# The expert stage of an AdaLN block: output groups, selection steps and the last unit's rows are placed elsewhere

## The chip, the cores and the metric

One core of a Trainium2 chip runs the whole program. The metric is the device time of one execution in microseconds. The kernel before has a median of 1168.9 us in three runs (1168.67 to 1169.73).

## The reference

The input is x of shape (4, 2048, 256). A first half (layer norm, a gated linear recurrence over the sequence, a projection, a residual) gives x1. The second half is an expert layer in which each expert picks its tokens:

```python
h = _layernorm(x, axis=-1) * (1 + cb) + sb
# _L0_ffn_ref
k = int(EXPERT_CAP * t / NUM_EXPERTS)                  # 2 * 2048 / 8 = 512
probs = softmax(einsum('ntd,de->nte', x, gate_w))
g, m = top_k(transpose(probs, (0, 2, 1)), k)           # per sample and expert
xin = x[m]
h = gelu(einsum('nekd,edf->nekf', xin, w1))            # 256 -> 1024
h = einsum('nekf,efd->nekd', h, w2)                    # 1024 -> 256
out = zeros.at[flat_idx].add(g[..., None] * h)         # summed per token
out = out.astype(bfloat16)
x = x + gb * out
```

There are 4 samples and 8 experts, so 32 pairs, each with 512 chosen tokens. The sum per token is rounded to bfloat16 once, before it is multiplied by gb and added to x1.

## The kernel before

The first half runs over 16 groups of 512 tokens and stores x1 with its statistics to DRAM (`xr_dram`); while it runs, the tokens of sample 0 are chosen. The expert stage then runs 32 **units** (u = 0 to 31), one pair of expert and sample each, in the order of `UNITS`: eight experts for sample 0, then samples 1 to 3. In this stage each engine has one list of instructions in a fixed order.

**One unit on TensorE** is `turn(u)` (L1739, the gathered rows are transposed), `layer2(u - 1, ...)` (L1763: four tiles of 128 tokens, 24 matmuls each) and `layer1(u)` (L1788: eight steps m of 6 matmuls, into four PSUM banks). Operands are split in a high and a low part, and three products are made of them. So the second layer's part of a unit is that of the unit before it. ScalarE does `turned_rows(u)` (L1512, L1518), the high parts of new weights (`split_hi`, L1552), `weigh(u - 1)` (L1530: second-layer tiles times the gates, into `rows_y`), `normalise(u + 1)` (L1559) and then, for each m, the gelu into `hf` (L1582, four buffers) and its high part into `hidT` (L1586). VectorE does `rows_lo` (L1642), `keep_gates`, the places for the token list of unit u + 2 (`slots_of`, `places_of`, L402), `split_lo` (L1603) and, for each m, `lo(u, m)` (L1655). TensorE's `make_list` (L420) turns the places to a list of 512 tokens, `keep_list` stores it, and GpSimd gathers the rows (`fetch`, L440) and adds weighed rows to the sums in DRAM (`add(u)`, L1461, waits for `f_y` and has four accumulating DMAs, one per tile).

**The choice** for samples 1 to 3 takes 30 rounds: VectorE compares all probabilities with a candidate (L217), TensorE sums the hits (L293), VectorE keeps or drops the bit. `PER_UNIT` deals the rounds to units 0 to 5, up to six each: three in the second layer's part (behind its tiles) and three in `layer1`. Unit 6 (`CHOSEN_IN`) has the rest: `ties` (L236 to L243), `select` (L249 to L259), `number` (L265, L267), `keep_slots` (L276 to L280), with small matmuls between them (`sum_ties` L298, `sum_selected` L304, `turn_slots` L311), and after that the list for unit 8, which `make_list` makes ahead of step m = 7.

**The output** is formed in 16 groups of 512 tokens, four for each sample (`FINISH_IN`: sample b in unit 28 + b). A group k takes `round_sum(k)` on ScalarE (L1541, sums to bfloat16) and `finish_sum(k)` on VectorE (L1609, times gb; L1613, plus x1). In the kernel before `along(u, m)` puts one group behind each odd m of `layer1`. SyncE's queue is in order: it loads x1 for five groups (L1431) and sums for four groups (L1426) ahead; then, for each k, it waits for the result, stores it (L1442), loads x1 of group k + 5 into a buffer whose store must have landed, and loads the sums of group k + 4. The load of a sample's first sums waits until the sample's last `add` has landed: `add(27)` for sample 1 (unit 29), `add(28)` for sample 2 (unit 30), `add(29)` for sample 3 (unit 31).

**Units 30 and 31** (`DIRECT`) do not add to DRAM. `fetch_sums(u)` gathers the sums (L1474) and x1 (L1477) of their tokens, and `direct(u, t)` on VectorE (L1628 to L1635) adds `rows_y`, rounds, multiplies and adds x1; `store_direct` on GpSimd scatters the rows to the output (L1489), after the stores of that sample's groups have landed. All eight `direct` calls stand behind the last `lo`, and ScalarE's `weigh(31)` is the last of its list.

## Time and profile before

| | us |
|---|---|
| median of 3 runs | 1168.9 |
| profiled execution, its time | 1173.53 |
| its span (first to last instruction of the program) | 1171.7 |
| TensorE busy | 1075.5 (92%) |
| VectorE / ScalarE / GpSimd busy | 741.6 / 756.4 / 428.3 |
| mean granted TensorE clock | 0.951 of 2.4 GHz |

The span is the profiled execution's from its first to its last instruction. A granted clock of 1.00 is 2.4 GHz and 0.50 is 1.2 GHz. The expert stage runs from about 360 us to the end; most of its units take between 23 and 25 us.

### The profile page before, as it was taken

To read this page: it belongs to the slowest core of one execution; us is meant where nothing else is said; L and a number is where in the kernel's file an instruction comes from. 1 tells how busy PE (TensorE), PEld (TensorE's weight loads), DVE (VectorE), ACT (ScalarE), POOL (GpSimd) and SP (SyncE) were. 2 spreads that over 40 slices of the span, in tenths; PEclk is the share of its full clock that TensorE was granted. 3 is DMA by queue.
4 is the path that set the end of the run, shared out by engine and by line. 5 is a ranking of instruction groups with operands and counts; after the bars stand their busy time and mean duration, and the time that the engine had idled before them with its cause. 6 is when DMAs were issued, how large, how long until landed. Compare 5 with 4: busy or idle time off the path is not lost.

```text
span 1171.7 us, 18741 instructions
## 1 busy us (share of the span) xinstructions
PE 1075.5 (92%) x6986; PEld 949.9 (81%) x6986; DVE 741.6 (63%) x1711; ACT 756.4 (65%) x1194; POOL 428.3 (37%) x384
## 2 busy tenths in 40 slices
PE   6579999999974999999999999999999999999993
PEld 5467878777863889988899889998999899988883
DVE  3658887989865788877545445545453554446665
ACT  2337666557615788776776677667776776676661
POOL 1012221212131345454443545454445453543542
PEclk8779998999976999999999999999999999999997
DMA  6004534221016545455522433334234432378971
GB/s 220 0 1 132 178 125 113 80 62 55 30 55 71 144 115 150 118 118 143 120 52 43 106 59 88 78 69 96 51 79 82 82 85 45 60 194 252 276 276 79
DMA packets 88443, 122.45 MB, mean 105 GB/s; under 512 B 17057, under 2 KB 74017, under 8 KB 87329
## 3 DMA queue, kind: packets, MB, share of 16 engines
q1 hardware_dynamic: 61456, 83.96, 22.4%
q0 software_dynamic: 24576, 36.37, 17.3%
q8 instruction: 55, 0.90, 0.3%
q10 hardware_dynamic: 2320, 0.93, 0.3%
q14 instruction: 36, 0.29, 0.1%
HBM read 78.96 MB, written 42.27 MB: 103 GB/s over the span
## 4 chain that ended last, share of the span: by engine, by line
PE 58%; DVE 6%; ACT 2%; issue 2%; POOL 1%; DMA 0%; POOLq 0%; ACTq 0%; DVEq 0%
PE psum L1763 29%; PE psum L1788 26%; PE psum L1739 2%; DVE w_raw L1609 1%; DVE hidT L1655 1%; DVE scratch L1613 1%; PE psum L420 1%; DVE w L1603 1%; ACT rows_in L1559 1%; ACT hf L1582 1%; POOL out_x L1489 1%; DVE place L402 0%; ACT acc L1541 0%; DVE res_t L1613 0%; DMA out_x<-scratch 0%
## 5 line engine op out<-in xcount | busy, mean ns | idle before, releaser
L1763 PE MATMUL psum<-w,hidT 128*128 128x256 f32 x3072 | 374.7, 284 | 11.7 <-DVE hidT L1655 11.7
L1763 PEld LDWEIGHTS psum<-w,hidT 128*128 128x128 f32 x3072 | 367.1, 192 | 13.4 <-DVE hidT L1655 13.1
L1788 PE MATMUL psum<-xT,w 128*128 128x512 f32 x1536 | 372.1, 398 | 0.3 <-DVE xT L1642 0.3
L1655 DVE TENSOR_TENSOR hidT<-hf,hidT 128x512 fp32r<-128x512 f32 x256 | 175.5, 692 | 265.9 <-ACT hidT L1586 265.7
L1788 PEld LDWEIGHTS psum<-xT,w 128*128 128x128 f32 x1536 | 285.8, 190 | 59.5 <-DVE xT L1642 0.7
L1461 POOL DMA_INDIRECT ffn_rows<-rows_y,idx_cur x120 | 205.4, 1711 | 229.5 <-issue 167.5
L440 POOL DMA_INDIRECT rows_in<-x_rows,idx_cur x128 | 138.3, 1081 | 187.2 <-DVE idx_cur L413 157.1
L1530 ACT ACTIVATE rows_y<-psum,g_cur 128x256 f32<-128x256 f32 x128 | 53.7, 469 | 190.7 <-PE psum L1763 190.7
L1586 ACT ACTIVATE hidT<-hf 128x512 fp32r<-128x512 f32 x256 | 161.8, 632 | 8.1
L1582 ACT ACTIVATE hf<-psum 128x512 f32<-128x512 f32 x256 | 150.6, 588 | 22.7 <-PE psum L1788 13.6
L760 ACT ACTIVATE ta<-psum,half_ba 128x512 f32<-128x512 f32 x32 | 20.3, 684 | 103.7 <-PE psum L1111 103.7
L684 POOL TENSOR_SCALAR ve<-x 128x4 f32<-128x4 f32 x16 | 3.7, 229 | 223.2 <-DVE x L826 223.2
L402 DVE TENSOR_TENSOR place<-row_id,slot_u 128x1024 bf16<-128x1024 bf16 x64 | 76.1, 1222 | 1.1
L1559 ACT ACTIVATE rows_in<-rows_in 128x256 f32<-128x256 f32 x128 | 66.3, 594 | 14.8 <-PEq L605 14.8
L1603 DVE TENSOR_TENSOR w<-w_raw,w 128x1024 fp32r<-128x1024 f32 x60 | 71.2, 1221 | 3.3 <-ACT w L1552 3.2
L1642 DVE TENSOR_TENSOR xT<-xf,xT 128x1024 fp32r<-128x1024 f32 x32 | 39.2, 1226 | 45.7 <-ACT xT L1518 45.7
L1111 PE MATMUL psum<-hT_z,Wa 128*128 128x512 f32 x192 | 54.9, 437 | 13.6 <-DVE hT_z L852 13.6
L1215 PE MATMUL psum<-Wout,hs 128*128 128x256 f32 x256 | 66.5, 392 | 0.0
L1552 ACT ACTIVATE w<-w_raw 128x1024 fp32r<-128x1024 f32 x60 | 59.7, 1045 | 8.4 <-DMA w_raw<-in_L_ffn_w 8.4
L1111 PEld LDWEIGHTS psum<-hT_z,Wa 128*128 128x128 f32 x192 | 38.4, 205 | 22.2 <-DVE hT_z L852 14.2
L1111 PE MATMUL psum<-hT_z,Wu 128*128 128x512 f32 x192 | 51.7, 414 | 0.0
L1215 PEld LDWEIGHTS psum<-Wout,hs 128*128 128x128 f32 x256 | 46.1, 198 | 5.2
(201 smaller groups left out, 1252.1 us busy)
## 6 DMA issues: line engine op xcount, KB each, us to landing
w_raw<-in_L_ffn_w SPq DMA_DIRECT2D x30, 1024.0 KB, 6.0
x_rows<-x SPq DMA_DIRECT2D x16, 516.0 KB, 3.8
x_buf<-in_L_attn_x SPq DMA_DIRECT2D x16, 512.0 KB, 5.9
ffn_rows<-scratch SPq DMA_DIRECT2D x8, 1024.0 KB, 8.3
w_raw<-ffn_rows SPq DMA_DIRECT2D x16, 512.0 KB, 8.9
scratch<-x_rows SPq DMA_DIRECT2D x12, 512.0 KB, 6.8
out_x<-scratch SPq DMA_DIRECT2D x12, 512.0 KB, 4.4
rows_in<-x_rows,idx_cur POOLq DMA_INDIRECT x136, 2.9
```

The lines of the kernel that those rows point to most:

```text
L402: dve.tensor_tensor(place[n][:, at, :], row_id[:].unsqueeze(1).to_broadcast([P, ST // 2, P]), slot_u[n][:, at, :].to_broadcast([P, ST // 2 ...
L440: pool.indirect_dma_start(rows_in[u % 2][:, t, :], None, xr_dram[b], bass.IndirectOffsetOnAxis(ap=idx_cur[u % 4][:, t:t + 1], axis=0))\
L1111: ins = pe.matmul(out_, stationary(qs, k), moving(qm, k), start=(first and j == 0), stop=(last and j == len(terms) - 1))
L1215: ins = pe.matmul(O_tok[:, t, :], hs[d % 2][:, k, t * P:(t + 1) * P], Wout[d // GB % 2][:, k, :], start=False, stop=(k == KD - 1))
L1461: pool.indirect_dma_start(acc_dram[b], bass.IndirectOffsetOnAxis(ap=idx_cur[u % 4][:, t:t + 1], axis=0), rows_y[u % 2][:, t, :], None, com ...
L1559: ins = act.activation(x_u[:, t, 0:D], x_u[:, t, 0:D], ACT.Identity, bias=x_u[:, t, D:D + 1], scale=x_u[:, t, D + 1:D + 2])
L1582: act.activation(hf[m % HF][:], H_bank[m % 4], ACT.Gelu_apprx_tanh).then_inc(f_hf, 1)
L1586: act.activation(hidT[0][:, m, :], hf[m % HF][:], ACT.Copy).then_inc(f_hh, 1)
L1603: dve.tensor_tensor(parts[1][:, at, :], raw[:, at, :], parts[0][:, at, :].bitcast(F32), ALU.subtract).then_inc(f_ws, 1)
L1655: dve.tensor_tensor(hidT[1][:, m, :], hf[m % HF][:], hidT[0][:, m, :].bitcast(F32), ALU.subtract).then_inc(f_hl, 1)
L1763: ins = pe.matmul(y_tile(u, t), hidT[qs][:, k, t * P:(t + 1) * P], w2_s[n % 2][qm][:, k, :], start=(x_ == 0), stop=(x_ == len(terms) - 1))
L1788: ins = pe.matmul(H_bank[m % 4], w1_s[n % 2][qs][:, k, m * P:(m + 1) * P], xT[qm][:, k, :], start=(x_ == 0), stop=(x_ == len(terms) - 1))
```

## The change

The four groups of a unit are taken out of `layer1` and put in the second layer's part: on ScalarE two ahead of `weigh`'s first half and two ahead of its second half, on VectorE one ahead of `rows_lo` and the others behind it. The rounds are dealt as 2, 6, 6, 6, 6, 4 (before: 3, 6, 6, 5, 5, 5). `ties` moves to unit 5 behind `lo(5, 2)`; in unit 6 `select`, `number`, `keep_slots` and the places for unit 8 stand in the second layer's part, with the small matmuls behind tiles 0, 2 and 3, and `make_list` ahead of m = 5. In unit 0 the `split_lo` of the next weights goes behind `lo(0, 7)`. Unit 30's `direct` calls go behind the odd `lo` of unit 31; unit 31's read the second layer's result in PSUM with one scalar_tensor_tensor, and ScalarE's `weigh(31)` is gone.

```diff
-        def along(u, m):
-            for b in range(B):
-                if u == FINISH_IN[b] and m % 2 == 1:
-                    return b * GB + m // 2
-            return None
+        def groups_in(u):
+            return [b * GB + j for b in range(B) if u == FINISH_IN[b] for j in range(GB)]
...
-        PER_UNIT = [3, 6, 6, 5, 5, 5]
+        PER_UNIT = [2, 6, 6, 6, 6, 4]
...
-            return [None] * (6 - PER_UNIT[u]) + [rounds_until(u) + j for j in range(PER_UNIT[u])]
+            here = [rounds_until(u) + j for j in range(PER_UNIT[u])]
+            return [None] * (6 - len(here)) + here if u == 0 else here + [None] * (6 - len(here))
...
-                def weigh(u):
-                    act.wait_ge(f_g, u + 1)
-                    if u >= 2:
-                        act.wait_ge(f_add[UNITS[u - 2][1]], 16 * CT * (turn_of(u - 2) + 1))
-                    for t in range(CT):
...
+                def weigh(u, half):
+                    if half == 0:
+                        act.wait_ge(f_g, u + 1)
+                        if u >= 2:
+                            act.wait_ge(f_add[UNITS[u - 2][1]], 16 * CT * (turn_of(u - 2) + 1))
+                    act.wait_ge(f_Y, 2 * u + half + 1)
+                    for t in range(half * CT // 2, (half + 1) * CT // 2):
                         ins = act.activation(rows_y[u % 2][:, t, :], y_tile(u, t), ACT.Copy, scale=g_cur[u % 2][:, t, 0:1])
...
+                    ins.then_inc(f_y, 1)
...
+                    sums = groups_in(u)
+                    for k in sums[:2]:
+                        round_sum(k)
                     if u >= 1:
-                        weigh(u - 1)
+                        weigh(u - 1, 0)
+                    for k in sums[2:]:
+                        round_sum(k)
+                    if u >= 1:
+                        weigh(u - 1, 1)
                         if u + 1 < NU:
                             normalise(u + 1)
...
-                        k = along(u, m)
-                        if k is not None:
-                            round_sum(k)
...
-                weigh(NU - 1)
...
+                    dve.wait_ge(f_ga[n], 16 * CT)
                     if u == NU - 1:
+                        if t % 2 == 0:
+                            dve.wait_ge(f_Yh, t // 2 + 1)
+                        else:
+                            dve.wait_ge(f_Y, 2 * u + t // 2 + 1)
+                        dve.scalar_tensor_tensor(out=o16[t % 2][:], in0=y_tile(u, t), scalar=g_cur[u % 2][:, t, 0:1],
+                                                 in1=acc_l[n][:, t, :], op0=ALU.mult, op1=ALU.add).then_inc(f_yd, 1)
                         dve.wait_ge(f_yd, t + 1)
                     else:
                         dve.wait_ge(f_y, 2 * u + t // 2 + 1)
-                    dve.wait_ge(f_ga[n], 16 * CT)
-                    dve.tensor_tensor(acc_l[n][:, t, :], acc_l[n][:, t, :], rows_y[n][:, t, :], ALU.add).then_inc(f_ds, 1)
-                    dve.wait_ge(f_ds, 3 * i + 1)
-                    dve.tensor_copy(o16[t % 2][:], acc_l[n][:, t, :]).then_inc(f_ds, 1)
-                    dve.wait_ge(f_ds, 3 * i + 2)
+                        dve.tensor_tensor(o16[t % 2][:], acc_l[n][:, t, :], rows_y[n][:, t, :], ALU.add).then_inc(f_yo, 1)
+                        dve.wait_ge(f_yo, t + 1)
                     dve.tensor_tensor(acc_l[n][:, t, :], o16[t % 2][:], gb_bc[:, b, :], ALU.mult).then_inc(f_ds, 1)
...
+                    sums = groups_in(u)
+                    for k in sums[:1]:
+                        finish_sum(k)
                     rows_lo(u)
                     keep_gates(u)
...
                     if late:
-                        chosen.ties()
-                    elif v:
+                        chosen.select()
+                        for w in work[:2]:
+                            split_lo(*w)
+                        chosen.number()
+                        for w in work[2:3]:
+                            split_lo(*w)
+                        chosen.keep_slots()
+                    if v:
                         slots_of(dve, v)
                         places_of(dve, v, 0)
+                    for k in sums[1:2]:
+                        finish_sum(k)
                     bits(n[0], n[1])
-                    if late:
-                        chosen.select()
-                    elif v:
+                    if v and not late:
                         places_of(dve, v, 1)
+                    for k in sums[2:3]:
+                        finish_sum(k)
                     bits(n[1], n[2])
...
+                    for k in sums[3:]:
+                        finish_sum(k)
                     bits(n[2], n[3])
...
+                        if v and late and m == 1:
+                            places_of(dve, v, 1)
+                        if u + 1 == CHOSEN_IN and m == 2:
+                            chosen.ties()
...
-                        k = along(u, m)
-                        if k is not None:
-                            finish_sum(k)
-                    if u == NU - 1:
-                        for d in DIRECT:
-                            rows_of_out(d)
-                            for t in range(CT):
-                                direct(d, t)
+                        if u == NU - 1 and m % 2 == 1:
+                            direct(u - 1, m // 2)
+                    if u == 0:
+                        for w in work[2:]:
+                            split_lo(*w)
+                for t in range(CT):
+                    direct(NU - 1, t)
...
-                        if v and m == (7 if late else 2):
+                        if v and m == (5 if late else 2):
                             make_list(pe, v)
-                        if late and m == 1:
-                            turn_slots(pe, 1)
...
-                        if u == CHOSEN_IN and t == 1:
+                        if u == CHOSEN_IN and t == 0:
+                            pe.wait_ge(f_xf, u + 1)
                             sum_ties(pe, 1)
+                        if u == CHOSEN_IN and t == 2:
+                            sum_selected(pe, 1)
                         if u == CHOSEN_IN and t == 3:
-                            sum_selected(pe, 1)
+                            turn_slots(pe, 1)
```

## Rows read from the trace of the kernel before

**Rows 1.** The page: the span, and the chain that ended last by engine

```profile
span 1171.7 us, 18741 instructions
...
PE 58%; DVE 6%; ACT 2%; issue 2%; POOL 1%; DMA 0%; POOLq 0%; ACTq 0%; DVEq 0%
```

**Rows 2.** Waits of TensorE, 1000 us to the end: us in total, times, longest

```profile
PE psum L1763 <- DVE hidT L1655: 9.3, 4, 2.4
```

**Rows 3.** Windows, TensorE alone: stretch, length, busy (count), clock, DMA share, GB/s

```profile
1064.20:1067.60 3.40, 3.40 (x16) 0.50 0.96 328
...
538.50:541.90 3.40, 3.40 (x14) 0.51 0.17 18
```

**Rows 4.** Timeline of TensorE, units 28 to 31: start, us, instruction, idle before

```profile
1035.59 11.14 PE L1763 MATMUL psum<-w,hidT 128*128 128x256 f32 x96
1046.57 2.91 PE L1788 MATMUL psum<-xT,w 128*128 128x512 f32 x12
...
1063.51 10.98 PE L1763 MATMUL psum<-w,hidT 128*128 128x256 f32 x78 [2.27 <-DVE hidT L1655]
1074.33 2.91 PE L1788 MATMUL psum<-xT,w 128*128 128x512 f32 x12
...
1129.49 11.17 PE L1788 MATMUL psum<-xT,w 128*128 128x512 f32 x48
```

**Rows 5.** Groups by line, 1046.6 to 1070 us: busy us, mean ns | idle before

```profile
L1655 DVE TENSOR_TENSOR hidT<-hf,hidT 128x512 fp32r<-128x512 f32 x8 | 5.3, 693 | 8.2 <-ACT hidT L1586 8.2
...
L1586 ACT ACTIVATE hidT<-hf 128x512 fp32r<-128x512 f32 x8 | 5.1, 632 | 0.3
...
L1609 DVE TENSOR_TENSOR w_raw<-acc,gb_bc 128x1024 f32<-128x1024 bf16 x4 | 4.9, 1220 | 0.3 <-ACT acc L1541 0.3
L1582 ACT ACTIVATE hf<-psum 128x512 f32<-128x512 f32 x8 | 4.6, 580 | 0.0
L1541 ACT ACTIVATE acc<-w_raw 128x1024 bf16<-128x1024 f32 x4 | 4.2, 1040 | 0.0
```

**Rows 6.** Timeline of TensorE and ScalarE, unit 0 and the start of unit 1

```profile
374.52 0.16 PE L293 MATMUL psum<-n_hit,same_e 128*128 128x3 bf16 x1 [2.11 <-DVE hit L217]
...
390.91 4.97 PE L1763 MATMUL psum<-w,hidT 128*128 128x256 f32 x27 [2.42 <-DVE hidT L1655]
...
386.79 1.99 ACT L1552 ACTIVATE w<-w_raw 128x1024 fp32r<-128x1024 f32 x2
...
390.14 1.06 ACT L1518 ACTIVATE xT<-xf 128x1024 fp32r<-128x1024 f32 x1
```

**Rows 7.** Timeline of TensorE, unit 6

```profile
518.75 0.18 PE L298 MATMUL psum<-n_hit,same_e 128*128 128x3 bf16 x1 [1.48 <-DVE n_eq L243]
...
535.23 0.36 PE L420 MATMUL psum<-vals_u,place 128*128 128x8 bf16 x8 [0.60 <-DVE place L402]
537.56 0.35 PE L420 MATMUL psum<-vals_u,place 128*128 128x8 bf16 x8 [1.98 <-DVE place L402]
```

**Rows 8.** Instructions of L1461, the one issued at 1050.24 us: issue to landing

```profile
DMA to landing us min/median/max: 3.9/3.9/3.9
```

**Rows 9.** Windows, all engines: stretch, length, PE, PEld, DVE, ACT, POOL, clock, DMA share, GB/s

```profile
1025.00:1040.00 15.00, 15.00 (x105) 13.05 (x104) 7.06 (x13) 13.02 (x22) 7.31 (x6) 1.00 1.06 340
...
1086.00:1102.00 16.00, 13.64 (x106) 13.39 (x104) 9.38 (x11) 7.48 (x12) 7.73 (x6) 0.89 1.00 339
```

**Rows 10.** The page, DMA issues: size, median us from issue to landing

```profile
w_raw<-ffn_rows SPq DMA_DIRECT2D x16, 512.0 KB, 8.9
```

**Rows 11.** Timelines of ScalarE, VectorE and GpSimd at the end; landing of L1489's DMAs

```profile
1156.30 0.47 ACT L1530 ACTIVATE rows_y<-psum,g_cur 128x256 f32<-128x256 f32 x1 [2.35 <-PE psum L1763]
...
1160.44 0.42 DVE L1635 TENSOR_TENSOR place<-place,rows_in 128x256 f32<-128x256 f32 x1
...
1161.68 0.96 POOL L1489 DMA_INDIRECT out_x<-place,idx_out  x1 [0.43 <-issue]
...
DMA to landing us min/median/max: 2.4/2.5/2.6
```

More of the change, by code:

```diff
@@ L1352, in adaln_kernel @@
         f_Yh = sem("last_y_tile_in_psum")
-        f_yd = sem("last_rows_y_tile_ready")
+        f_yd = sem("last_y_tile_summed")
+        f_yo = sem("direct_sums_ready")
         f_io = sem("out_rows_known")
@@ L1626, in direct @@
                         dve.wait_ge(f_y, 2 * u + t // 2 + 1)
-                    dve.wait_ge(f_ga[n], 16 * CT)
-                    dve.tensor_tensor(acc_l[n][:, t, :], acc_l[n][:, t, :], rows_y[n][:, t, :], ALU.add).then_inc(f_ds, 1)
-                    dve.wait_ge(f_ds, 3 * i + 1)
-                    dve.tensor_copy(o16[t % 2][:], acc_l[n][:, t, :]).then_inc(f_ds, 1)
-                    dve.wait_ge(f_ds, 3 * i + 2)
+                        dve.tensor_tensor(o16[t % 2][:], acc_l[n][:, t, :], rows_y[n][:, t, :], ALU.add).then_inc(f_yo, 1)
+                        dve.wait_ge(f_yo, t + 1)
                     dve.tensor_tensor(acc_l[n][:, t, :], o16[t % 2][:], gb_bc[:, b, :], ALU.mult).then_inc(f_ds, 1)
-                    dve.wait_ge(f_ds, 3 * i + 3)
+                    dve.wait_ge(f_ds, i + 1)
                     dve.wait_ge(f_gx[n], 16 * CT)
@@ L1679, in _ @@
                     if late:
-                        chosen.ties()
-                    elif v:
+                        chosen.select()
[6 more added lines that the diff above has]
+                    if v:
                         slots_of(dve, v)
                         places_of(dve, v, 0)
+                    for k in sums[1:2]:
+                        finish_sum(k)
                     bits(n[0], n[1])
-                    if late:
-                        chosen.select()
-                    elif v:
+                    if v and not late:
                         places_of(dve, v, 1)
+                    for k in sums[2:3]:
+                        finish_sum(k)
                     bits(n[1], n[2])
-                    if late:
-                        chosen.number()
-                    for w in work[:2]:
-                        split_lo(*w)
+                    if not late:
+                        for w in work[:2]:
+                            split_lo(*w)
+                    for k in sums[3:]:
+                        finish_sum(k)
                     bits(n[2], n[3])
-                    if u:
+                    if u and not late:
                         for w in work[2:3]:
                             split_lo(*w)
+                    if u in DIRECT:
+                        rows_of_out(u)
                     for m in range(KH):
@@ L1705, in _ @@
                             bits(n[5], None)
-                        if late and m == 0:
-                            chosen.keep_slots()
-                            slots_of(dve, v)
-                        if late and m in (2, 4):
-                            places_of(dve, v, m // 2 - 1)
+                        if v and late and m == 1:
+                            places_of(dve, v, 1)
+                        if u + 1 == CHOSEN_IN and m == 2:
+                            chosen.ties()
                         if v and m == (5 if late else 3):
                             keep_list(dve, v)
-                        if m == 6:
-                            for w in work[3:] if u else work[2:]:
+                        if u and m == 6:
+                            for w in work[3:]:
                                 split_lo(*w)
-                        k = along(u, m)
-                        if k is not None:
-                            finish_sum(k)
-                    if u == NU - 1:
-                        for d in DIRECT:
-                            rows_of_out(d)
-                            for t in range(CT):
-                                direct(d, t)
+                        if u == NU - 1 and m % 2 == 1:
+                            direct(u - 1, m // 2)
+                    if u == 0:
+                        for w in work[2:]:
+                            split_lo(*w)
+                for t in range(CT):
+                    direct(NU - 1, t)
             @block.tensor
```

7 lines of the change are left out of this document (removed).

## The prediction

> **What bounds the kernel now.** I read the page first: TensorE is on 58% of the chain that ended last, no other engine on more than 6% [rows 1]. The timeline of TensorE then shows one unit after another without a gap from 391 us to 1060 us, but for unit 6. So in the middle only what takes TensorE's time away counts, and the places to look at are its waits. There are three, and the end.
>
> *Units 28 to 31.* Each has one wait of `layer2` for the low part of the hidden layer, 9.3 us in four [rows 2]. Unit 28 runs from 1046.57 to 1074.33 us, 27.76 us [rows 4]. The wait is 2.27 of it. Behind it 78 matmuls take 10.98 us, where 96 take 11.14 in the unit before, so 78 should take 9.05: 1.93 us more [rows 4]. The window there shows why: 3.4 us at a granted clock of 0.50, 1.2 GHz, right behind the wait [rows 3]. So the wait costs 4.2 us, and a unit without it is 27.76 - 4.20 = 23.56 us (23.2 without a list to make). Four of them: 16.8, say 17 us. The cause is ScalarE in `layer1`: 0.58 and 0.63 us for each m, and 1.04 us for the group at each second m, is about 1.7 us for each m [rows 5]; TensorE takes 11.17 / 8 = 1.40 [rows 4].
>
> *Unit 6.* TensorE waits 1.48 us for the ties and 0.60 + 1.98 us for the places [rows 7], and the clock is at half for 3.4 us from 538.5 [rows 3], another 1.7. Together 5.8 us.
>
> *Unit 0.* It waits 2.11 us for the first comparison and 2.42 us for the last low part, which stands behind two `split_lo` on VectorE [rows 6]. The 27 matmuls behind the second wait take 4.97 us where 27 / 96 of 11.14 is 3.13: 1.84 for the clock, and I count 1.7 for the first wait too. Together 8.1 us.
>
> *The end.* The last tile leaves TensorE at about 1156.26 (ScalarE's `weigh` starts at 1156.30). VectorE is then still behind with `direct` and ends at 1160.86; GpSimd issues the last scatter 0.82 us later, at 1161.68 [rows 11]; the span ends at 1171.7. So 5.4 us lie between the last tile and the last scatter, and 10.0 behind that, which I leave as they are.
>
> **Unit 0.** With round 0 at position 4, the compare stands behind `lo(0)` and TensorE asks for its hits behind m = 3: the 2.11 us go. `split_lo` behind `lo(7)`: the 2.42 us go. What is late next is ScalarE's list: after the last gelu it has `split_hi` (1.99 us), two passes for `xf` and 1.06 for `xT` [rows 6], and VectorE needs `rows_lo` and a compare behind them, some 2 us, before TensorE may sum the first hits of unit 1, behind its second tile. I lay the order out from the end of m = 1: TensorE would reach that point some 7.7 us earlier than today, and the hits are there 5.8 us ahead of the time at which it takes them today. So I expect a new wait of about 2 us there, and in half of the cases the clock behind it (1.7). 5.8 less half of 1.7 is 5.0, which I take. Bounds: 2.4 (only the second wait goes) and 8.1.
>
> **Unit 6.** `ties` in unit 5 costs VectorE under 3 us between `lo(2)` and `lo(3)`; four `hf` buffers and the 0.7 us that it has free in each m [rows 4, 5] take it up. The selection then runs beside the 11 us of `layer2(5)`, and the second half of the places follows `lo(1)`. `make_list` at m = 5 has it about then: I keep a wait of 0.4 us. 5.8 - 0.4 = 5.4. Bounds: 1.5 (only the wait for the ties goes; the places are as late as today) and 5.8.
>
> **Units 28 to 31: the compute.** Groups now lie beside `layer2`, 11 us long, in which ScalarE had two weighings to do and VectorE little. Four casts are 4.2 us, four times two passes of 1.22 are 9.8 us on VectorE [rows 5]. With `rows_lo` and the places VectorE ends some 7.5 us behind the start of `layer1` and starts the `lo` up to 3.3 us late; it needs 0.62 for each where 1.40 come, so TensorE does not feel it. By compute alone all 17 us are won.
>
> **The loads are what is late next.** SyncE is in order, and the load of a sample's first sums waits for the last `add` of the second-last unit. In unit 28 that add is issued at 1050.24 and lands 3.9 us later [rows 8], at 1054.1: 7.5 us behind the start of `layer1`. Today the load comes after it anyway, as results come through `layer1` one by one. In the new order the four results are ready before, and SyncE stands at this load with everything behind it. From the landing on, the fourth sums are the tenth transfer: sums; store, x1, sums; three times. Ten times 0.524 MB [rows 10] is 5.24 MB; the gathers of the next unit are 4 x 128 x 1064 B = 0.54, the first two adds 0.26: 6.05 MB. With the DMA engines busy all the time they move 339 to 340 GB/s [rows 9]: 17.8 us. A scatter of 0.13 MB needs 2.5 us to land, of which 0.96 is its issue and 0.4 its bytes [rows 11], so 1.1 us for completion. The burst takes 19 us.
>
> The fourth cast then ends 7.5 + 19.0 + 1.04 = 27.5 us behind the start of `layer1`, and the next `layer1` starts at 23.56: ScalarE is 4.0 us late for the second half of `weigh`. It is covered in part: behind it come six passes of some 0.48 [rows 11], so the first gelu starts 2.9 us into `layer1`, and TensorE needs its bank at m = 4, 5.6 to 6.0 us in. With 0.58 for the gelu 2.3 us are free.
> - Unit 29: late 4.0, TensorE waits 1.7.
> - Unit 30: the add of unit 28 was as late as ScalarE, the unit has moved by 1.7 only, so 2.3 remain, and the new burst adds 4.0: late 6.3, wait 4.0.
> - Unit 31: nine transfers, but 16 gathers of `fetch_sums` beside them: 4.72 + 2.1 = 6.8 MB, 20.1 + 1.1 = 21.2 us. Late by 7.5 + 21.2 + 1.04 - 23.2 + 2.3 = 8.8. VectorE has the last group (2.4) to finish, then eight `lo` of 0.62 and three `direct` of 1.3: `lo(7)` is there 8.8 + 2.4 + 8.9 = 20.1 us in, and `layer2` wants it at 11.0 + 2.5 = 13.5. Wait 6.6.
>
> Sum 12.3, and 1.7 for a clock at half behind the last (behind the others the chain isn't TensorE's). 17 - 14 = 3 us are won. One microsecond more or less in a burst is three in the sum. Bounds for the stage: 17 if a burst takes 16.5 us or less; and 3 us lost for a burst of 21.
>
> The Trainium skill, "DMA: Bandwidth & Descriptors", section Specifications, puts a core's share of HBM at about 358 GB/s, whichever queues ask for it. [Rows 9] agree, 5% below it. By the page's figure a burst would be an estimated 18 us and the stage 3 us better. The page speaks against any hope that a burst is hidden by having the queue full.
>
> **The end.** Unit 30's `direct` lie in `layer1` of unit 31. Unit 31's tile 3 has three passes in place of ScalarE's one and VectorE's four: two of 0.42 [rows 11], and the scalar_tensor_tensor from PSUM, which the trace does not show at this size. Nearest are 0.42 (VectorE, SBUF) and 0.47 (ScalarE, PSUM, rows 11); I take 0.5, at most twice that. 1.4, then 0.8 to the issue: 2.2 in place of 5.4, so 3.2 are won (2.7 to 3.3). The stores of groups 8 to 15 have landed by then. If they have not, GpSimd waits as today for 17 us beside other work, and 0 to 3 us come back.
>
> **The sum.** 5.0 + 5.4 + 3.0 + 3.2 = 16.6 us off the profiled execution: 1173.5 - 16.6 = 1156.9. That execution was 4.6 us above the median of the runs (1168.9), which I carry over: 1152.3 us.
>
> **The rivals.**
> - *The loads do not bind.* A burst of 16.5 us is 6.05 MB at 393 GB/s. Against it: the two windows at 339 to 340 [rows 9]. For it: those windows hold mixed traffic, ScalarE may have cover that I did not see, and sums wait in four buffers. The stage gives 17: 30.6 in all, 1138.3 us.
> - *Longer bursts.* At 300 GB/s a burst is 21.3 us and the stage loses 4: gain 9.6, 1159.3 us.
> - *Slower than before.* The same loop, load to cast to `weigh` to add to load, closes over SyncE's queue, with the adds' read and write and the gathers taking more than their bytes. The rest of the change gives 13.6, so it is slower from a loss of 13.6 in the stage on, 16.6 more than I forecast, a burst of 19 + 16.6 / 3 = 24.5 us. That is 6.05 MB at 259 GB/s. The median sums' load needs 8.9 us to land [rows 10], so there is queueing, but neither window of [rows 9] is near that. At a burst of 25.5 us: 1172 us.
> - *Unit 6 keeps its wait for the places* (VectorE late by the weights' `split_lo` between `select` and `number`): the gain is 3.9 less, 1156.2 us.
>
> **Chances.** Forecast with its own range 1147 to 1158 (bursts of 17.5 to 20.5 us, unit 0 between 3 and 7): 0.48. Unit 6 keeps its wait: 0.06. Loads do not bind, 1137 to 1146: 0.23. Longer bursts, 1158 to 1166: 0.14. Slower: 0.05. The 0.04 left are for what I have not seen: 0.03 for no change and 0.01 for slower. A measurement of this kernel can tell 0.2% (2.3 us) from no change. Range 1139 to 1162: it takes in the first rival but for its last microsecond and most of the second. Faster 0.91, same 0.03, slower 0.06.
>
> **What would show it.** Right: no wait of `layer2` for `hidT` in unit 28; ScalarE idle ahead of L1541 on a DMA in units 29 to 31; TensorE's waits there growing, 2, 4, 7 us; DMA windows at share 1.0 in the second half of each unit; unit 6 without a wait above 1 us; TensorE waiting at L293 at the start of unit 1; the last scatter 2.2 us behind the last matmul. Wrong: fourth casts on time (then the first rival), a wait in unit 6 or a half clock there, or a last scatter that waits for a store.

## The result, and the profile after

The changed kernel takes 1154.06 us (median of 4 runs, 1152.96 to 1157.07) where the kernel before takes 1168.84: a ratio of 0.9867, 95% interval 0.9842 to 0.9893. It is 14.8 us faster; forecast were 1152.3 us, and 16.6 us of gain. The profiled execution took 1153.6 us, its span is 1151.8.

I measured both traces at the same marks: the first turning of gathered rows, the start of layer 1 of units 7 and 28, the last matmul, the end.

| us | before | after | difference | forecast |
|---|---|---|---|---|
| start to first turning | 361.5 | 358.2 | -3.3 | 0 |
| to layer 1 of unit 7 (units 0 to 6) | 191.5 | 180.9 | -10.6 | -10.4 |
| to layer 1 of unit 28 | 493.5 | 493.5 | 0.0 | 0 |
| to the last matmul (units 28 to 31) | 109.7 | 106.8 | -2.9 | -3.0 |
| to the end | 15.4 | 12.4 | -3.1 | -3.2 |

(The differences are taken before rounding.) The 3.3 us of the first row are not the change's; the last section shows where they come from. Without them the spans differ by 16.6. That this is the forecast to the tenth is luck: these are two single executions, and the first units of the kernel before take between 189.5 and 191.5 us in the five traces that have them unchanged (before, e1, e3, e8, e10). The medians differ by 14.8.

The page after, busy time by engine and the chain that ended last by engine:

```profile
PE 1065.7 (93%) x6986; PEld 941.2 (82%) x6986; DVE 741.2 (64%) x1703; ACT 755.3 (66%) x1190; POOL 432.2 (38%) x384
...
PE 59%; DMA 4%; ACT 2%; issue 1%; DVE 1%; SPq 1%; POOL 0%; ACTq 0%; POOLq 0%; DVEq 0%
```

Against [rows 1] two things moved: VectorE fell from 6% of the chain to 1%, and transfers came from 0% to 4%. VectorE is out of the way, SyncE's transfers have come into it.

Waits of TensorE from 980 us to the end (us in total, times, longest), and under it its timeline in the same stretch, only the rows with a wait of a `layer1` or `layer2` ahead of them:

```profile
PE psum L1799 <- ACT hf L1583: 9.6, 3, 5.6
PE psum L1776 <- DVE hidT L1656: 0.4, 1, 0.4
```

```profile
1064.26 5.79 PE L1799 MATMUL psum<-xT,w 128*128 128x512 f32 x24 [1.74 <-ACT hf L1583]
1073.69 8.79 PE L1776 MATMUL psum<-w,hidT 128*128 128x256 f32 x75 [0.37 <-DVE hidT L1656]
1093.53 7.54 PE L1799 MATMUL psum<-xT,w 128*128 128x512 f32 x24 [5.55 <-ACT hf L1583]
1120.68 7.37 PE L1799 MATMUL psum<-xT,w 128*128 128x512 f32 x24 [2.35 <-ACT hf L1583]
```

This is the answer to [rows 2]: before, four waits of `layer2` for VectorE's low parts, 9.3 us; after, none in unit 28 and three waits of `layer1`, at m = 4, for ScalarE's gelu, 9.6 us. The sum of waiting is the same, its cause another. The 5.79 us of the first row are 24 matmuls at full clock (24 / 48 of 11.17 is 5.59); the 7.54 and 7.37 are not. What ScalarE waits for, 1032 to 1140 us, and its late work in unit 30:

```profile
ACT acc L1535 <- DMA w_raw<-ffn_rows: 28.1, 9, 4.9
```

```profile
1084.06 1.06 ACT L1535 ACTIVATE acc<-w_raw 128x1024 bf16<-128x1024 f32 x1 [2.18 <-DMA w_raw<-ffn_rows]
1089.26 1.06 ACT L1535 ACTIVATE acc<-w_raw 128x1024 bf16<-128x1024 f32 x1 [4.14 <-DMA w_raw<-ffn_rows]
1090.22 0.82 ACT L1527 ACTIVATE rows_y<-psum,g_cur 128x256 f32<-128x256 f32 x2
1090.93 2.07 ACT L1553 ACTIVATE rows_in<-rows_in 128x256 f32<-128x256 f32 x4
1092.89 0.58 ACT L1583 ACTIVATE hf<-psum 128x512 f32<-128x512 f32 x1
```

Read it downwards: the load of the fourth sums lands at 1089.2, the cast, two weighings and four passes follow without a gap, the first gelu ends at 1093.5, and TensorE goes on at 1093.53 (the timeline above). The transfers are busy meanwhile. Windows of all engines (stretch, length, busy and count of PE, PEld, DVE, ACT, POOL; clock, DMA share, GB/s) in the bursts of units 29 to 31:

```profile
1045.00:1060.00 15.00, 15.00 (x128) 14.24 (x127) 11.55 (x14) 6.78 (x10) 6.43 (x5) 1.00 1.06 378
1075.00:1090.00 15.00, 12.98 (x90) 11.64 (x89) 8.57 (x8) 4.88 (x7) 4.84 (x2) 1.00 1.01 346
1100.00:1118.00 18.00, 18.00 (x133) 16.78 (x131) 10.26 (x11) 8.41 (x12) 12.31 (x12) 1.00 1.00 371
```

Unit 6 has no wait of TensorE left (500 to 560 us), where [rows 7] had three. Unit 1 has the new one that was forecast; timeline of TensorE there:

```profile
386.09 0.16 PE L293 MATMUL psum<-n_hit,same_e 128*128 128x3 bf16 x1 [1.83 <-DVE hit L217]
386.11 4.39 PE L1776 MATMUL psum<-w,hidT 128*128 128x256 f32 x24
390.31 0.23 PE L293 MATMUL psum<-n_hit,same_e 128*128 128x3 bf16 x1
390.40 3.25 PE L1776 MATMUL psum<-w,hidT 128*128 128x256 f32 x24
```

A quarter of the 11.14 us of [rows 4] is 2.8; the first 24 matmuls took 4.39, at half clock. And the end, VectorE and GpSimd, last tile (last matmul at 1139.44):

```profile
1139.55 0.48 DVE L1626 SCALAR_TENSOR_TENSOR o<-psum,g_cur,place 128x256 bf16<-128x256 f32 x1 [1.32 <-PE psum L1776]
1140.07 0.43 DVE L1633 TENSOR_TENSOR place<-o,gb_bc 128x256 f32<-128x256 bf16 x1
1140.53 0.43 DVE L1636 TENSOR_TENSOR place<-place,rows_in 128x256 f32<-128x256 f32 x1
1141.77 0.96 POOL L1488 DMA_INDIRECT out_x<-place,idx_out  x1 [1.76 <-DVE place L1636]
```

Three passes, then the scatter 2.3 us behind the last matmul, where [rows 11] had 5.4.

### The profile page after: what moved, and what is told of

It reads as the page before. It is cut to its first block, busy times and chain, and to the rows that moved or that the text cites. A ratio compares the mean times of both kernels' runs of the same rounds, so it can differ in the third digit from the quotient of the medians.

```text
span 1151.8 us, 18728 instructions
## 1 busy us (share of the span) xinstructions
PE 1065.7 (93%) x6986; PEld 941.2 (82%) x6986; DVE 741.2 (64%) x1703; ACT 755.3 (66%) x1190; POOL 432.2 (38%) x384
## 4 chain that ended last, share of the span: by engine, by line
PE 59%; DMA 4%; ACT 2%; issue 1%; DVE 1%; SPq 1%; POOL 0%; ACTq 0%; POOLq 0%; DVEq 0%
PE psum L1799 28%; PE psum L1776 28%; DMA w_raw<-ffn_rows 2%; PE psum L1752 2%; DMA out_x<-scratch 2%; PE psum L420 1%; DMA ffn_rows<-rows_y,idx_cur 1%; ACT rows_in L1553 1%; ACT hf L1583 0%; SPq L1425 0%; ACT rows_y L1527 0%; ACT xf L1511 0%; DVE xT L1643 0%; DVE w L1600 0%; SPq L1430 0%
## 5 line engine op out<-in xcount | busy, mean ns | idle before, releaser
L1776 PE MATMUL psum<-w,hidT 128*128 128x256 f32 x3072 | 367.0, 281 | 0.4 <-DVE hidT L1656 0.4
L1776 PEld LDWEIGHTS psum<-w,hidT 128*128 128x128 f32 x3072 | 360.2, 189 | 1.0 <-DVE hidT L1656 0.8
L1460 POOL DMA_INDIRECT ffn_rows<-rows_y,idx_cur x120 | 210.9, 1758 | 230.0 <-issue 164.4
L1546 ACT ACTIVATE w<-w_raw 128x1024 fp32r<-128x1024 f32 x60 | 59.9, 1045 | 10.5 <-DMA w_raw<-in_L_ffn_w 10.5
L1215 PE MATMUL psum<-Wout,hs 128*128 128x256 f32 x256 | 64.1, 381 | 0.0
```

The lines of the kernel that those rows point to most:

```text
L1215: ins = pe.matmul(O_tok[:, t, :], hs[d % 2][:, k, t * P:(t + 1) * P], Wout[d // GB % 2][:, k, :], start=False, stop=(k == KD - 1))
L1460: pool.indirect_dma_start(acc_dram[b], bass.IndirectOffsetOnAxis(ap=idx_cur[u % 4][:, t:t + 1], axis=0), rows_y[u % 2][:, t, :], None, com ...
L1776: ins = pe.matmul(y_tile(u, t), hidT[qs][:, k, t * P:(t + 1) * P], w2_s[n % 2][qm][:, k, :], start=(x_ == 0), stop=(x_ == len(terms) - 1))
```

## The experiments

All ratios are to the kernel before, with their 95% intervals. "The stage" is units 28 to 31, "the tail" is what lies behind the last matmul, both from the profiled executions.

**The three parts, each alone on the kernel before.** First the groups:

```diff
+                    sums = groups_in(u)
+                    for k in sums[:2]:
+                        round_sum(k)
                     if u >= 1:
-                        weigh(u - 1)
+                        weigh(u - 1, 0)
+                    for k in sums[2:]:
+                        round_sum(k)
+                    if u >= 1:
+                        weigh(u - 1, 1)
...
-                        k = along(u, m)
-                        if k is not None:
-                            finish_sum(k)
```

> The kernel before with the groups alone moved into the second layer's part. My theory: the 17 us of TensorE's waits in units 28 to 31 go, but bursts of about 20 us behind the last add take some 14 back (as in the trace of the whole change, units 28 to 31 net 2.8 us): about 1166.0 us. Rival: the groups carry most of the gain of the whole change and the other parts little: about 1155 us. Second rival: without the other parts' time the loop of loads is no tighter than the old waits: 1168.8 us, no change.

Measured 1166.22 us, 0.9977 (0.9952 to 1.0002): near the expected 1166.0, but the interval takes in no change too, so what follows rests on the trace. The stage fell from 109.7 to 105.2 us, and TensorE's waits there are of the kind of the changed kernel:

```profile
PE psum L1796 <- ACT hf L1587: 7.7, 3, 5.1
PE psum L1771 <- DVE hidT L1657: 1.4, 3, 0.5
```

9.1 us of waiting in place of 9.3, so the 4.5 us gained are nearly all clock: one wait above 2 us in place of four, and a mean granted clock of 0.97 over the stage where it was 0.94.

Then the rounds, ties, selection and `split_lo`:

```diff
-        PER_UNIT = [3, 6, 6, 5, 5, 5]
+        PER_UNIT = [2, 6, 6, 6, 6, 4]
...
                     if late:
-                        chosen.ties()
+                        chosen.select()
```

> The kernel before with only the rounds, ties, selection and split_lo moved. My theory: unit 0 with the start of unit 1 gives 4.8 us, unit 6 with its clock 5.8, nothing downstream takes it back: 1168.8 - 10.6 = 1158.2 us. Rival: TensorE catches up but the gathers for unit 8 or the weights' loads come late instead, and less than half of it is left: 1164 us.

Measured 1160.59 us, 0.9919 (0.9896 to 0.9943). Units 0 to 6 took 180.3 us, 11.2 less. I had expected 1158.2 us and a gain of 10.6; the ratio gives 9.5. The mechanism stands, and by itself it is most of the change's gain.

Last the finish from the accumulators:

```diff
-                weigh(NU - 1)
...
+                        dve.scalar_tensor_tensor(out=o16[t % 2][:], in0=y_tile(u, t), scalar=g_cur[u % 2][:, t, 0:1],
+                                                 in1=acc_l[n][:, t, :], op0=ALU.mult, op1=ALU.add).then_inc(f_yd, 1)
```

> The kernel before with only unit 31's rows finished from PSUM and three passes in place of four (unit 30's direct calls stay behind the last lo). My theory: the last scatter starts 2.2 us behind the last matmul in place of 5.4: 1165.6 us. Rival: unit 30's four direct calls, still behind the last lo, keep VectorE late at the end, or the scatters' own distance of 1.4 us sets it: 1168 us.

Measured 1172.16 us, 1.0023 (1.0001 to 1.0046): my expectation fell. The tail is 12.4 us, 3.0 shorter as expected, but the stage is 5.0 longer. Waits of TensorE, then VectorE's timeline (two of its rows):

```profile
PE psum L1767 <- DVE hidT L1659: 9.3, 4, 2.4
PE psum L1767 <- DVE o L1629: 3.0, 1, 3.0
```

```profile
1154.06 0.18 DVE L1617 TENSOR_SCALAR idx_out<-idx_cur 128x4 int32<-128x4 int32 x1
1154.15 0.47 DVE L1629 SCALAR_TENSOR_TENSOR o<-psum,g_cur,place 128x256 bf16<-128x256 f32 x1
```

The accumulators are read by VectorE now, not by ScalarE, so tile 2, which takes tile 0's place in PSUM, must wait for VectorE; and that still has unit 30's four `direct` calls ahead (1149.0 to 1154.1). TensorE waits 3.04 us, and the 48 matmuls behind it take 7.32 us in place of 5.57. So the part needs unit 30's calls elsewhere. I tried that too:

```diff
-                    if u == NU - 1:
-                        for d in DIRECT:
-                            rows_of_out(d)
-                            for t in range(CT):
-                                direct(d, t)
+                        if u == NU - 1 and m % 2 == 1:
+                            direct(u - 1, m // 2)
```

> The kernel before with the end part whole and nothing else of the change: e3_last_rows_alone (last unit's rows finished from the accumulators, three passes in place of four) and, beside it, unit 30's four direct calls inside layer 1 of unit 31 as the change has them. e3 was 3.1 us shorter behind the last matmul and 5.0 us longer in the stage of units 28 to 31, with 3.04 us of waiting for VectorE's sum in layer 2 of unit 31. If that wait is unit 30's calls standing ahead of it, the 3.1 us stay and the 5.0 go: 1168.8 - 3.1 = about 1165.7 us. Rival: the calls are only moved and hold up layer 1 of unit 31 by as much, where finish_sum(12) to (15) stand too: 1170 to 1172 us.

Measured 1169.84 us, 1.0002 (0.9986 to 1.0018). The tail is again 12.4, the stage 113.5, 3.8 longer. The wait for tile 2 is gone, and others have grown:

```profile
PE psum L1768 <- DVE hidT L1659: 12.4, 5, 3.6
```

Unit 31 has 1.75 and 3.63 us of them. In the kernel before VectorE has a group behind each odd m of that layer already; the calls come on top. The rival was right in its mechanism, and nearly in its time. The trace of the kernel before shows why the order alone can't help: there VectorE's list bounds the end. From its last `lo` at 1144.90 us it goes through one group and all eight `direct` calls without a wait until 1160.86, and comes to the last tile 2.9 us after TensorE has left it (1159.20, 1156.26). A call that is put ahead of a `lo` delays that `lo`, and TensorE with it.

So the end part is worth nothing that can be told by itself. By their ratios the three parts, with the end part as in e8, give 2.7, 9.5 and -0.2 us alone, 12.0 in sum, and the whole 15.5. The 3.5 us between them would fit an end part that pays once the groups are out of `layer1`, but each of the four numbers has an interval of 2 to 3 us to either side, and no run takes the end part alone out of the changed kernel. By the traces, stage and tail together are 120.1 us in e1 (105.2 and 14.9) and 119.2 in the changed kernel (106.8 and 12.4): 2.5 us of tail are won and 1.7 of the stage lost. How much of that loss the end part causes is open.

**The burst.** The prediction had SyncE's burst as what remains. First one more transfer ahead of each of its later loads of sums, on the changed kernel:

```diff
                     if k + AHEAD_A < NG:
+                        if k % GB:
+                            sp.wait_ge(o_sp, 16 * (k - 1 - k // GB))
+                            sp.dma_start(runs(acc_dram[0], 0), runs(xr_dram[k // GB], k % GB * GT)[:, :, 0:D]).then_inc(o_sp, 16)
                         load_acc(k + AHEAD_A)
```

> The changed kernel with three more transfers of 0.52 MB in each of the three bursts of SyncE (DRAM to DRAM, rows of xr_dram into the summed rows of batch 0 that nothing reads by then, each issued just ahead of the load of sums k+4 where k is not 0, 4, 8). Nothing else waits for them. This adds to the suspected cost by itself. If the burst of SyncE is what the last cast of the sums, and behind it layer 1 of units 29 to 31, ends on, each burst grows by 3 x about 1.6 us = 4.8 us and the three stages by most of that, some 14 us: about 1168 us. The rival, that the loads are hidden and TensorE's waits of 1.7, 5.6 and 2.4 us come from ScalarE's own work, gives 1154 to 1157 us.

Measured 1174.92 us, 1.0036 (1.0020 to 1.0051). The stage is 126.9 us, 20.0 longer; from the last add's landing to the fourth sums' the bursts take 6.2, 6.6 and 6.9 us more. Waits of TensorE, ScalarE's group of casts (idle behind the bar), and SyncE's own wait for the added copies:

```profile
PE psum L1803 <- ACT hf L1587: 27.4, 3, 10.5
...
L1539 ACT ACTIVATE acc<-w_raw 128x1024 bf16<-128x1024 f32 x12 | 12.6, 1052 | 47.2 <-DMA w_raw<-ffn_rows 47.2
...
SPq L1448 <- DMA ffn_rows<-x_rows: 23.5, 6, 5.6
```

The same three waits, 17.8 us longer. What is added to a burst comes back in the time in full, so the path from SyncE's burst over the last cast to TensorE is shown. The 2.2 us for each copy, in place of my 1.6, are no price of a transfer: the edit makes each copy but the first wait until the one before it has landed, and SyncE stood 23.5 us in six such waits.

Then the opposite, the same transfers in another order: the four loads of sums behind all four stores and loads of x1, so that SyncE doesn't stand at the first load of sums, waiting for the last add, with stores behind it that are ready.

```diff
-                    if k + AHEAD_A < NG:
-                        load_acc(k + AHEAD_A)
+                    if k % GB == GB - 1 and k + 1 < NG:
+                        for j in range(k + 1, k + 1 + GB):
+                            load_acc(j)
```

> The changed kernel with SyncE's order changed: a sample's results are all stored and x1 loaded first, and the four loads of the next sample's sums, which wait for the last add, come behind them. Same bytes, same compute. My theory: only four transfers lie between the add's landing and the last sums, so these come some 8 to 10 us behind the add in place of 20, ScalarE waits for none of them, and TensorE's waits of 1.7, 5.6 and 2.4 us in units 29 to 31 go with their clock and late gelus: units 28 to 31 take 92.5 us in place of 106.9, and the time is 1154.1 - 14.4 = 1139.7 us. Rival, the DMA engines' rate is what binds and not the order: the sums still land late, under 3 us are won, 1151 us or more.

Measured 1147.04 us, 0.9796 (0.9748 to 0.9845); the stage 99.2 us, 7.7 less. (The interval just touches the changed kernel's, 0.9842 to 0.9893; e6 below, with the same order, lies clear of it.) From the landing of the last add to that of the fourth sums it takes 10.5, 12.6 and 8.8 us, where the changed kernel takes 19.1, 20.0 and 19.9. Of the 13.3 us lost to waits and clock, 7.7 are gone; I had expected all. The adds land later, now that stores and x1 loads run beside them (the last one of `add(27)` 8.6 us after its issue in place of 4.3), and what is left are other waits:

```profile
PE psum L420 <- DVE place L402: 1.9, 1, 1.9
PE psum L1777 <- DVE hidT L1657: 1.5, 2, 1.2
PE psum L1800 <- DVE xT L1644: 1.1, 1, 1.1
```

VectorE stood 17.5 us in three waits for a rounded group, with `rows_lo` and the places behind it. The same order on the kernel before, alone:

> The kernel before with SyncE's order of e4 (each burst: stores and loads of x1 of all four groups, then the four loads of sums) and nothing else. If the burst binds only since the change asks for the sums in layer 2's part, nothing is gained here: in the kernel before, VectorE stood 1.0 us for rounded sums in the last stage and the groups are asked for later, so 1166 to 1171 us. Rival: the adds of units 27 to 29 and TensorE's waits in the kernel before hang on the same transfers, and the order alone takes a part of the 17 us: 1160 us.

Measured 1169.97 us, 0.9990 (0.9969 to 1.0012): nothing that can be told. TensorE's waits are the same 9.3 us in four as in [rows 2]; the stage is 3.1 us shorter and the tail 1.5 longer. There the burst wasn't the bound; with the groups moved it is (e1 has the same waits for the gelu).

**What is left.** On e4, `split_hi` and `split_lo` of the next expert's weights moved from the end of unit 0 to unit 1:

```diff
-                    for n, q in work[:4 if u else 2]:
+                    for n, q in (splits_in(0)[2:] if u == 1 else []) + work[:4 if u else 2]:
                         split_hi(n, q)
...
                     bits(None, n[0])
+                    if u == 1:
+                        for w in splits_in(0)[2:]:
+                            split_lo(*w)
```

> e4_sums_loads_last, and of the work that the change gathered in unit 0 the last split_hi and split_lo of the next expert's weights moved on into unit 1. In the changed kernel TensorE waits 1.83 us in unit 1 at the turning of the list and runs its next 24 matmuls at half clock (4.39 us in place of 2.6). If VectorE's and ScalarE's work left over from unit 0 makes that wait, both go: 3.5 us under e4, about 1143.5 us. If the wait is the chain of the choice itself (count, compare, turn) nothing moves: 1147 us.

Measured 1147.13 us, 0.9804 (0.9779 to 0.9828): nothing in the time. But the wait is not the same one. TensorE in unit 1, and VectorE's moved work:

```profile
384.06 0.16 PE L293 MATMUL psum<-n_hit,same_e 128*128 128x3 bf16 x1
384.09 2.97 PE L1774 MATMUL psum<-w,hidT 128*128 128x256 f32 x24
389.40 0.17 PE L293 MATMUL psum<-n_hit,same_e 128*128 128x3 bf16 x1 [2.34 <-DVE hit L217]
389.42 4.45 PE L1774 MATMUL psum<-w,hidT 128*128 128x256 f32 x24
```

```profile
383.83 2.36 DVE L1598 TENSOR_TENSOR w<-w_raw,w 128x1024 fp32r<-128x1024 f32 x2
```

The wait of the changed kernel, 1.83 us at the count of the first round (not at the turning of the list, as the expectation has it), is gone: without `split_hi` ahead of them ScalarE's rows are ready 2.0 us earlier, and so is VectorE's first compare. The splits did make that wait, as the prediction had it. The new one stands at the second count: the edit puts `split_lo`, 2.36 us, between the first compare and the second. The wait is handed on, with the half clock behind it.

VectorE's order in units 29 to 31:

```diff
-                    for k in sums[:1]:
-                        finish_sum(k)
                     rows_lo(u)
                     keep_gates(u)
...
-                    for k in sums[1:2]:
+                    for k in sums[:2]:
                         finish_sum(k)
```

> e6_splits_in_unit1 with VectorE's first finished group of units 29 to 31 put behind rows_lo, keep_gates and the places of the list, where e4 had it ahead of them. In e4 three waits of TensorE are left in the end stage, 1.9 us for the places of unit 29's list, 1.1 us for the lower halves of unit 31's rows and 1.5 us for a hidden tile, and VectorE stood 17.5 us in 3 waits for rounded sums ahead of them. If that order makes the first two, they go: 3.0 us and the half clock behind them, about 1.5 us, 4.5 us under e6, about 1139 us. Rival: the wait is only handed on to the hidden tiles of layer 1, since the groups then stand closer to them: 0 to 1 us under e6.

Measured 1145.39 us, 0.9777 (0.9751 to 0.9803), where I had expected 1139. The stage is 95.85 us, 2.7 under e6. The waits for places and for `xT` (0.5 and 0.8 us in e6's execution) are gone, and those of `layer2` for `hidT` grew from 1.5 to 2.2 us in three: the rival's handing on, in part. So 0.6 of the 2.7 us are waits; the rest is the granted clock, 1.00 over the stage where e6 had 0.98. The intervals of e6 and e7 don't touch the changed kernel's (0.9842 to 0.9893). e7 has the lowest median, some 9 us below it; its step over e6 and e4 is not told by the times, the intervals overlap.

Last, in unit 1, the decision of the first round ahead of the next list's slots and places:

```diff
+                    if u == 1:
+                        bits(n[0], n[1])
                     if v:
                         slots_of(dve, v)
                         places_of(dve, v, 0)
```

> e7_rows_ahead with one line moved in unit 1: VectorE decides the first round of the choice and compares for the second before it does the slots and the first places of the next list, not behind them. e6 showed that TensorE's wait there (2.2 us at the count of the second round, the clock at half behind it for some 6 us) is not the splits. If it is VectorE's slots and places, 1.9 us of work between the two compares, the wait falls to about 0.4 us and the clock stays: 1.8 + about 1.7 = 3.5 us under e7, about 1142 us, and the stretch from the first turn to layer 1 of unit 7 falls from 181.8 to about 178.3. Rival: the decision then waits for TensorE's sum itself, and the wait stays above 1.5 us: no change.

Measured 1145.74 us, 0.9776 (0.9747 to 0.9806): no gain. The wait of 2.2 us is gone, 0.54 are left at that count, so what stands between the two compares made it (the moved `split_lo` as well as slots and places). But it is handed on: waits of TensorE in units 1 to 6, e7 first, then e9:

```profile
PE psum L293 <- DVE hit L217: 3.6, 3, 2.2
```

```profile
PE psum L293 <- DVE hit L217: 3.2, 5, 1.1
```

VectorE has more work in unit 1 than fits (from 383 to 395 us of e9 it is busy 11.75 of 12 us); the same 3 us come out at the later rounds. Units 0 to 6 take 181.1 us in place of 181.8. There was no clock to win back either: in e7's execution, unlike e6's, it stayed at 1.00 behind that wait. (In e6 it was below 1.00 from 389.5 to 394.5 us, at a mean of 0.66, which is some 3.4 us at half and not the 6 of the expectation.)

## Why the prediction was right, point by point

- **Unit 0**, forecast 5.0. Layer 1 of unit 1 starts at 393.53 us in place of 401.67, 8.1 earlier; less the 3.3 of the first half that is 4.8. Both waits of [rows 6] are gone, the new one at the start of unit 1 is 1.83 us for the forecast 2, and the clock fell behind it, which I had put at one half. Its cause was right too: e6 takes ScalarE's splits away and the wait at the first count goes. That it would be handed on when removed (e6, e9) I did not see. The size is looser than 4.8 against 5.0 looks: from the first turning to layer 1 of unit 1 the unchanged code took 38.2 to 40.1 us in five executions, and the changed 34.3 to 35.3 in four (e2, the changed kernel, e4, e5).
- **Unit 6**, forecast 5.4. The rest of units 0 to 6 gave 10.6 - 4.8 = 5.8. No wait was left, not even the 0.4 us I kept, and in the stretch of [rows 3] the clock is 1.00:

```profile
538.50:541.90 3.40, 3.40 (x20) 1.00 0.93 298
```

- **Compute of units 28 to 31.** Unit 28 takes 23.69 us without a wait, forecast 23.56. The 17 us that the waits of the kernel before cost with their clock were some 16.1: it has 109.7 us, where e7's matmuls at a clock of 1.00 fill 93.6. That 0.9 too much stands against 0.8 too much on the side of the losses.
- **The bursts**, forecast 19, 19, 21.2 us. They took 19.1, 20.0, 19.9, at 346 to 378 GB/s, the upper end above the 339 to 340 that I had read. The page "DMA: Bandwidth & Descriptors" of the Trainium skill (section Specifications) gives some 358 GB/s for a core; this trace has 378 in a window of 15 us, so its figure is no hard ceiling here. Nor does the page make it one for this case: its section Bandwidth says that each core gets about 358 with both cores of a pair streaming, and that its own higher numbers are those of a single core. One core runs here, so the page doesn't speak against a shorter burst as the prediction took it to; the windows of [rows 9] do.
- **The waits**, forecast 1.7, 4.0, 6.6 us; measured 1.74, 5.55, 2.35 and a 0.37: 10.0 in place of 12.3. Two sizes were off. *Unit 30:* the last add of unit 28 landed 13.0 us behind the start of layer 1, where I had 9.8. I let unit 29's wait of 1.7 move the whole unit, but it lies inside its layer 1, at m = 4, behind the mark from which I counted; with the burst a microsecond longer the cast is 8.0 us late, not 6.3. *Unit 31:* I had the wait at `layer2`, for `lo(7)`. It came at m = 4, for the gelu, as in the other units, and moved `layer2` by itself: 2.35 us and 1.8 for the clock, so that `lo(7)` was wanted at 17.6 and not 13.5 us. The last pair of low parts ended at 1130.6, 17.9 us in, and no wait shows. The step that counted both waits apart left out that the first covers the second. So the sign that I gave, waits growing as 2, 4, 7 us, didn't come. ScalarE had no rows to normalise there either (2.07 us in the rows above), so the gelu came earlier.
- **The clock.** I put 1.7 behind the last wait and none behind the others, since there the chain is ScalarE's. It fell behind the 5.55 and the 2.35, not behind the 1.74. TensorE is busy 96.8 us in the stage, in e7, at a clock of 1.00, 93.6: so 3.2 us, not 1.7. Windows of TensorE, behind the waits in units 29 and 30:

```profile
1061.00:1065.00 4.00, 2.26 (x10) 1.00 0.24 78
...
1092.00:1097.00 5.00, 3.47 (x8) 0.50 0.36 48
```

  10.0 + 3.2 = 13.2 us lost, forecast 14.0. The nearness is partly luck: the waits were 2.3 less, the clock 1.5 more.
- **The tail**, forecast 3.2. Measured 3.1; the scalar_tensor_tensor from PSUM takes 0.48 us for the assumed 0.5. But e3 and e8 show that these 3.1 us are not the part's own: without the groups moved, the stage pays 5.0 or 3.8 us for them. The prediction added the parts as if each stood by itself; that the sum came out for the whole doesn't show that each term did. It also split stage and tail at the last matmul. In the kernel before VectorE's list, not TensorE's, leads to the end (see e8), so that boundary moves without the end: in e2 the stage is 1.6 us shorter and the tail 1.9 longer. The two rows together, 5.9 us against 6.2 forecast, are the sounder comparison. GpSimd's wait of 17 us before its first scatter is VectorE's too: the profile names a store, but the scatter comes 1.0 us behind the first `direct` call (1150.64, 1149.63), as it does in e1, where the profile names VectorE.
- **The offset.** I carried over 4.6 us between the profiled execution and the median. The profiled one after is 0.5 us below its median. 3.3 of the 4.6 were the later start of the first turning, below; the other 1.3 and these 0.5 are the 1.8 us by which the forecast gain is above that of the medians.
- **The rivals.** That the loads do not bind is refuted by e5 (what was added to the bursts came back in full) and e4. A lengthening burst and the closing loop did not come, though e5 shows how near it is: 6.2 to 6.9 us more in a burst, near the 5.5 where I had put the turn, and the kernel is slower than before (1.0020 to 1.0051).

## What to carry to other kernels

When compute moves out of the way, the queue behind it is next: lay out who waits for whose landing, transfer by transfer, and put first what is ready, so that a transfer that must wait for another engine has nothing ready behind it. Give parts their price only together with what they need: here the finish from PSUM shortens the tail by 3 us wherever it stands, and without the moved groups the stage takes them back. And where an engine has no slack in a unit, as VectorE in unit 1, a wait taken away comes back at the next thing that it owes: when an edit leaves the time alone, look whether the wait is still the same one before acquitting what was moved (e6).

## What the runs showed of the hardware

**The same code, the same wait, two clocks.** The first half is the same in all twelve kernels, but the first turning starts at 358.1 to 359.2 us in some profiled executions and at 361.5 to 362.7 in others (the kernel before among them). Between the changed kernel and e7, which are 4.2 us apart, 1.7 are there by 110 us. The rest is here, TensorE in the changed kernel, then in e7:

```profile
331.20 0.36 PE L1213 MATMUL psum<-bias_rows,pick 128*128 128x256 f32 x1 [2.18 <-DVE x L894]
331.40 1.02 PE L1215 MATMUL psum<-Wout,hs 128*128 128x256 f32 x4
```

```profile
332.93 0.55 PE L1213 MATMUL psum<-bias_rows,pick 128*128 128x256 f32 x1 [2.18 <-DVE x L894]
333.28 1.91 PE L1215 MATMUL psum<-Wout,hs 128*128 128x256 f32 x4
...
333.00:336.00 3.00, 3.00 (x8) 0.50 0.00 0
```

The wait is 2.18 us in both. In one execution the four matmuls behind it take 1.02 us, in the other 1.91, at a granted clock of 0.50; by the next list the gap between the two has grown from 1.7 to 4.2 us. The kernel before is like e7 here, with a clock of 0.69 from 328 to 334 us. It is so in the expert stage too. Behind the 1.83 us of waiting at the first count of unit 1 the clock fell in the changed kernel; in e5, whose code is the same there, it did not:

```profile
391.17 0.16 PE L293 MATMUL psum<-n_hit,same_e 128*128 128x3 bf16 x1 [2.13 <-DVE hit L217]
391.19 3.07 PE L1780 MATMUL psum<-w,hidT 128*128 128x256 f32 x24
```

At the second count it fell behind 2.34 us in e6 (24 matmuls in 4.45 us) and not behind 2.24 us in e7 (2.99 us); and in e9 it fell behind waits of 1.08 and 1.24 us with 1.22 us of matmuls between them. Waits of this size have a price of some 2 us that comes or doesn't, so a forecast should give it a chance, as I did in unit 0 only. The Trainium skill, "TensorE: Matmul & The Clock Gate", Part 1, calls the number of slow matmuls at a kernel's start run-variable for one kernel. These traces show such a thing in the middle of one too.

**Transfers beside adds.** In the changed kernel the last two accumulating DMAs of `add(27)` to `add(29)`, for which SyncE's queue stands waiting, land 3.9 to 4.7 us after issue. The first two of `add(28)` and `add(29)`, issued while a burst runs, take 7.5 to 8.7 us, and in e4, with stores and loads of x1 beside all of them, the four of `add(29)` take 5.1 to 10.2 us. Their 0.13 MB do not tell this: their landing goes by the traffic that they stand in.
